# Two more tables and a second chain of scatters for the expert sums of a transformer layer

## The reference, cut to what matters

```python
x = x + layernorm(attention(layernorm(x)))          # 16 query heads, 4 key/value heads, causal
h = layernorm(x).reshape(4096, 256)
topk_w, topk_ids = grouped_topk(h @ gate_w, bias)   # 6 of 64 experts for each token, in 4 of 8 groups
# every expert takes at most 48 tokens (CAP), the earliest ones; the others get nothing from it
buf = zeros((64, 48, 256)).at[expert, slot].set(h[token])
e = silu(einsum('ech,ehf->ecf', buf, w_gate)) * einsum('ech,ehf->ecf', buf, w_up)
out = einsum('ecf,efh->ech', e, w_down)
y = segment_sum(out[expert, slot] * w, token)       # each token adds up what its experts gave it
shared = (silu(h @ ws_gate) * (h @ ws_up)) @ ws_down
x = x + layernorm(y + shared)
```

## Time and profile before

| | |
|---|---|
| median of 3 runs | 2156.44 us |
| the runs | 2150.07, 2156.80, 2156.44 us |
| the profiled execution, its own time | 2158.23 us |
| its span (first to last instruction) | 2156.4 us |
| PE busy | 1927.5 us (89% of the span) |
| DVE, ACT, POOL busy | 1333.7, 1149.5, 1293.5 us |
| attention | 0 to 1861 us |
| `last_quad` | 1861 to 1924 us |
| 32 pairs of experts | 1924 to 2097 us |
| tail | 2097 to 2156 us |

### The profile page before, as it was taken

The page is one execution under the profiler, slowest core; times in us unless marked ns, Lnnn a source line. Parts: engine busy times, 40 slices in busy tenths (PEclk is TensorE's granted clock), DMA queues, the critical chain, the costliest instruction groups (busy, mean ns, idle before and its releaser), DMA issues. The chain is left out here.

```text
span 2156.4 us, 34575 instructions
## 1 busy us (share of the span) xinstructions
PE 1927.5 (89%) x12006; PEld 1631.8 (76%) x12006; DVE 1333.7 (62%) x3172; ACT 1149.5 (53%) x2604; POOL 1293.5 (60%) x1055
## 2 busy tenths in 40 slices
PE   3899999999999999998999999999999999679940
PEld 2788888887788888887888888877888888447730
DVE  1466666666666677676667677766666777642217
ACT  2466665655556565655565655565655555222213
POOL 5666766675657574856585766666666655124533
PEclk9999999999999999999999999999999999885555
DMA  4000000001010100000100100011001000595226
GB/s 168 16 25 21 6 21 6 21 6 46 26 52 1 35 11 21 11 26 30 55 21 6 40 6 25 6 50 35 21 6 40 16 1 11 192 356 170 49 54 210
DMA packets 68587, 103.35 MB, mean 48 GB/s; under 512 B 9350, under 2 KB 49236, under 8 KB 67392
## 3 DMA queue, kind: packets, MB, share of 16 engines
q1 hardware_dynamic: 56816, 84.23, 11.6%
q0 software_dynamic: 7248, 12.72, 2.6%
q10 hardware_dynamic: 4352, 4.20, 0.6%
HBM read 73.47 MB, written 30.04 MB: 48 GB/s over the span
## 5 line engine op out<-in xcount | busy, mean ns | idle before, releaser
L536 PE MATMUL s_ps<-kT,q 128*128 128x512 f32 (+3 forms) x2304 | 596.6, 377 | 11.3 <-ACT probs L900 10.0
L779 DVE TENSOR_TENSOR pT<-t_ps,pT 128x512 fp32r<-128x512 f32 (+3 forms) x768 | 401.5, 550 | 329.8 <-ACT pT L911 328.7
L536 PEld LDWEIGHTS s_ps<-kT,q 128*128 128x128 f32 x2304 | 407.4, 194 | 56.0 <-ACT probs L900 15.7
L561 PE MATMUL av_ps<-pT,v 128*128 128x512 f32 x1728 | 437.1, 399 | 0.0
L1049 POOL TENSOR_TENSOR rope<-raw,sinT 64x512 f32<-64x512 f32 x320 | 411.1, 1285 | 24.6
L766 DVE TENSOR_REDUCE neg_max<-s_ps 128x1 f32<-128x640 f32 (+7 forms) x512 | 383.8, 750 | 65.8 <-PE s_ps L536 59.9
L900 ACT ACTIVATE probs<-s_ps,neg_max 128x640 f32<-128x640 f32 (+7 forms) x512 | 381.6, 745 | 66.5 <-DVE neg_max L766 65.1
L911 ACT ACTIVATE pT<-t_ps 128x512 fp32r<-128x512 f32 (+3 forms) x768 | 348.3, 489 | 127.5 <-PE t_ps L546 122.1
L1046 POOL TENSOR_TENSOR cosed<-raw,cosT 128x512 f32<-128x512 f32 x160 | 206.3, 1290 | 278.4 <-ACT raw L872 270.1
L561 PEld LDWEIGHTS av_ps<-pT,v 128*128 128x128 f32 x1728 | 315.9, 190 | 59.7
L546 PE MATMUL t_ps<-k_ident,probs 128*128 128x128 f32 x2304 | 341.9, 275 | 14.7 <-ACT probs L900 8.2
(11 more groups left out here) (193 smaller groups left out, 1934.6 us busy)
## 6 DMA issues: line engine op xcount, KB each, us to landing
w_early<-in_expert_w SPq DMA_DIRECT2D x5, 2560.0 KB, 29.3
w_staged<-in_wpack SPq DMA_DIRECT2D x47, 256.0 KB, 2.8
w_staged<-in_wpack SPq DMA_DIRECT2D x16, 512.0 KB, 3.6
w_early<-sums SPq DMA_DIRECT2D x16, 512.0 KB, 8.8
e_w_late<-in_expert_w SPq DMA_DIRECT2D x3, 2560.0 KB, 20.3
k_xw<-in_x SPq DMA_DIRECT2D x4, 1024.0 KB, 5.7
k_xb<-in_x SPq DMA_DIRECT2D x4, 1024.0 KB, 5.9
sums<-y POOLq DMA_DIRECT2D x4, 1024.0 KB, 8.7
```

The source lines that it names most:

```text
L536: last = pe.matmul(out, q[:, macro % 2, a, h, int(big)], kT[:, g % 2, s, lo:hi], start=(n == 0), stop=(n == 2))
L561: last = pe.matmul(av_ps[:], v[:, g % 2, a, j], pT[:, s, part_slot(p) + j], start=(j == 0 and n == 0), stop=(j == blocks - 1 and n == 2))
L779: dve.tensor_tensor(lo, t_ps[n % 2][:, 0:count * P].rearrange("p (j n) -> p j n", n=P), hi.bitcast(F32), ALU.subtract).then_inc(t_lo, 1)
```

## The change

- `sums` has four tables. At step `s == 40` of the attention ACT waits for the stores of the zeros and then copies table 1, which is all zeros, to tables 2 and 3 by two DMAs from DRAM to DRAM, 4.24 MB each. SP waits for them at the end of the block.
- Of the first 22 pairs (`TURNS = 11`) the odd ones add to tables 2 and 3, with a semaphore `added[1]` of their own; the even ones and all of the last ten add to tables 0 and 1 (`added[0]`). A scatter waits only for the scatter before it of its own chain. So two scatters can be under way in the first 22 pairs, and one in the last ten. `to_row` takes three instructions for each half instead of one.
- When the eleven odd scatters have landed, SP loads tables 2 and 3 (16 DMAs of 512 KB) while the last ten pairs run, and DVE adds them, one unit in each of its last eight steps (`joined`).
- After the last scatter SP loads tables 0 and 1 as before, 16 DMAs, table 0 now to a part of `w_late` and table 1 to where table 3 lay. POOL adds `m2` (tables 2 and 3) to `m0`; DVE adds `m1` to it, by a linked instruction ahead of the statistics of each unit.
- One semaphore of `w_in` covers two weight loads, so a wait is for 16 experts.

```diff
@@ attention, scalar
+                if s == 40:
+                    act.wait_ge(zeros_out, 16 * (B + 3))
+                    for n in (2, 3):
+                        act.dma_start(sums[n], sums[1]).then_inc(zeros_copied, 16)
...
+TURNS = 11
+
+def in_second(j):
+    return j % 2 == 1 and j < 2 * TURNS
+
+def scattered_earlier(j):
+    return sum(in_second(i) == in_second(j) for i in range(j))
...
@@ last_quad, vector
-            dve.tensor_scalar(index.to_row[0:64], c_ps[1][0:64, 0:EXPERTS // 2], -1.0, FAR, ALU.mult, ALU.add)
-            dve.tensor_scalar(index.to_row[64:128], c_ps[1][64:128, 0:EXPERTS // 2], -1.0, FAR + TABLE, ALU.mult, ALU.add)
+            second, first = slice(1, 2 * TURNS, 2), (slice(0, 2 * TURNS, 2), slice(2 * TURNS, EXPERTS // 2))
+            for i in range(2):
+                half = slice(64 * i, 64 * i + 64)
+                for cols, table in ((second, 2 + i), (first[0], i), (first[1], i)):
+                    dve.tensor_scalar(index.to_row[half, cols], c_ps[1][half, cols], -1.0, FAR + table * TABLE, ALU.mult, ALU.add)
...
@@ experts
-        x1, m0, m1 = (flat[:, i * SIZE:(i + 1) * SIZE].rearrange("p (t n) -> p t n", n=HID) for i in range(3))
+        x1, m2, m3 = (flat[:, i * SIZE:(i + 1) * SIZE].rearrange("p (t n) -> p t n", n=HID) for i in range(3))
+        m0, m1 = w_late[:].rearrange("p e n -> p (e n)")[:, 0:SIZE].rearrange("p (t n) -> p t n", n=HID), m3
+        def landed(j):
+            return added[in_second(j)], 16 * (scattered_earlier(j) + 1)
@@ experts, sync
             sp.wait_ge(y_ready, last_pair(2))
-            sp.wait_ge(added, 16 * PAIRS)
+            sp.wait_ge(added[1], 16 * TURNS)
             for u in range(UNITS):
                 first = u * UNIT * P
+                for dst, table in ((m2, 2 * TABLE), (m3, 3 * TABLE)):
+                    sp.dma_start(unit(dst, u), tiles(sums[table + first:table + first + UNIT * P])).then_inc(loaded[u], 16)
+            sp.wait_ge(y_ready, PAIRS)
+            sp.wait_ge(added[0], 16 * (PAIRS - TURNS))
+            for u in range(UNITS):
+                first = u * UNIT * P
+                sp.wait_ge(joined, u + 1)
                 for dst, table in ((m0, 0), (m1, TABLE)):
                     sp.dma_start(unit(dst, u), tiles(sums[table + first:table + first + UNIT * P])).then_inc(loaded[u], 16)
@@ experts, gpsimd
-                    if j:
-                        pool.wait_ge(added, 16 * j)
+                    if scattered_earlier(j):
+                        pool.wait_ge(added[in_second(j)], 16 * scattered_earlier(j))
...
-                pool.wait_ge(loaded[u], 32)
-                pool.tensor_tensor(unit(m0, u), unit(m0, u), unit(m1, u), ALU.add).then_inc(summed, 1)
+                pool.wait_ge(loaded[u], 64)
+                pool.tensor_tensor(unit(m0, u), unit(m0, u), unit(m2, u), ALU.add).then_inc(summed, 1)
@@ experts, vector
                 if s >= 2:
                     odd(s - 2)
+                u = s - (PAIRS + 2 - UNITS)
+                if u >= 0:
+                    dve.wait_ge(loaded[u], 32)
+                    dve.tensor_tensor(unit(m2, u), unit(m2, u), unit(m3, u), ALU.add).then_inc(joined, 1)
...
             for u in range(UNITS):
                 dve.wait_ge(summed, u + 1)
+                link(dve.tensor_tensor(unit(m0, u), unit(m0, u), unit(m1, u), ALU.add))
@@ experts, vector and scalar, odd(j) and even(j)
-                    wait_ge(added, 16 * (j - Y_RING + 1))
+                    wait_ge(*landed(j - Y_RING))
@@ experts, tensor
-                if (2 * j) % LOADS == 0:
-                    pe.wait_ge(w_in[2 * j // LOADS], 16)
+                if j % LOADS == 0:
+                    pe.wait_ge(w_in[j // LOADS], 32)
@@ build
-    sums = nc.dram_tensor("sums", (2 * TABLE, HID), F32).ap()
+    sums = nc.dram_tensor("sums", (4 * TABLE, HID), F32).ap()
```

More of the change, by code:

```diff
@@ L325, in attention @@
         table_ready, table_read = sem("table_ready"), sem("table_read")
-        zeroed, zeros_out = sem("zeroed"), sem("zeros_out")
+        zeroed, zeros_out, zeros_copied = sem("zeroed"), sem("zeros_out"), sem("zeros_copied")
         kv_in, q_in, o_in = sem("kv_in"), sem("q_in"), sem("o_in")
@@ L453, in _ @@
             sp.wait_ge(weight_out, 32 * (QUADS - 2))
+            sp.wait_ge(zeros_copied, 32)
         @block.tensor
@@ L1255, in _ @@
                 sp.dma_start(w_early[:, n * LOADS:(n + 1) * LOADS],
-                             consts["expert_w"][n * LOADS:(n + 1) * LOADS].rearrange("e p n -> p e n")).then_inc(w_in[n], 16)
+                             consts["expert_w"][n * LOADS:(n + 1) * LOADS].rearrange("e p n -> p e n")).then_inc(w_in[n // 2], 16)
         @block.tensor
@@ L1557, in experts @@
         gu_ready, tanh_done, act_done, h_done = sem("gu_ready"), sem("tanh_done"), sem("act_done"), sem("h_done")
-        y_ready, y_even, y_odd, added = sem("y_ready"), sem("y_even"), sem("y_odd"), sem("added")
+        y_ready, y_even, y_odd = sem("y_ready"), sem("y_even"), sem("y_odd")
+        added, joined = [sem(f"added{n}") for n in range(2)], sem("joined")
         x1_in = sem("x1_in")
@@ L1585, in _ @@
                 at = n * LOADS - EARLY
-                sp.dma_start(w_late[:, at:at + LOADS], consts["expert_w"][n * LOADS:(n + 1) * LOADS].rearrange("e p n -> p e n")).then_inc(w_in[n], 16)
+                sp.dma_start(w_late[:, at:at + LOADS], consts["expert_w"][n * LOADS:(n + 1) * LOADS].rearrange("e p n -> p e n")).then_inc(w_in[n // 2], 16)
             sp.wait_ge(y_ready, last_pair(0))
@@ L1612, in _ @@
                     pool.wait_ge(y_odd, j + 1)
-                    if j:
-                        pool.wait_ge(added, 16 * j)
+                    if scattered_earlier(j):
+                        pool.wait_ge(added[in_second(j)], 16 * scattered_earlier(j))
                     pool.indirect_dma_start(sums, bass.IndirectOffsetOnAxis(to_row[:, j:j + 1], 0), y[:, j % Y_RING], None,
-                                            bounds_check=2 * TABLE - 1, oob_is_err=False, compute_op=ALU.add).then_inc(added, 16)
+                                            bounds_check=4 * TABLE - 1, oob_is_err=False, compute_op=ALU.add).then_inc(added[in_second(j)], 16)
             for u in range(UNITS):
-                pool.wait_ge(loaded[u], 32)
-                pool.tensor_tensor(unit(m0, u), unit(m0, u), unit(m1, u), ALU.add).then_inc(summed, 1)
-            pool.wait_ge(added, 16 * PAIRS)
+                pool.wait_ge(loaded[u], 64)
+                pool.tensor_tensor(unit(m0, u), unit(m0, u), unit(m2, u), ALU.add).then_inc(summed, 1)
+            for n, count in enumerate((PAIRS - TURNS, TURNS)):
+                pool.wait_ge(added[n], 16 * count)
         @block.vector
@@ L1638, in odd @@
                 if j >= Y_RING:
-                    dve.wait_ge(added, 16 * (j - Y_RING + 1))
+                    dve.wait_ge(*landed(j - Y_RING))
                 at = HID + 2 * j + 1
@@ L1695, in even @@
                 if j >= Y_RING:
-                    act.wait_ge(added, 16 * (j - Y_RING + 1))
+                    act.wait_ge(*landed(j - Y_RING))
                 at = HID + 2 * j
@@ L1770, in build @@
         kept = Kept(lambda name, shape, dt=F32: ctx.enter_context(nc.sbuf_tensor("k_" + name, shape, dt)))
-        attention(nc, args, x, wpack, x1_rows, rows, [sums[0:TABLE], sums[TABLE:2 * TABLE]], x2t_rows, kept)
+        attention(nc, args, x, wpack, x1_rows, rows, [sums[n * TABLE:(n + 1) * TABLE] for n in range(4)], x2t_rows, kept)
         index = Index(lambda name, shape, dt=F32: ctx.enter_context(nc.sbuf_tensor("i_" + name, shape, dt)))
         w_early = ctx.enter_context(nc.sbuf_tensor("w_early", [P, EARLY, PACK], F32))
-        w_in = [ctx.enter_context(nc.semaphore(f"w_in{n}")) for n in range(EXPERTS // LOADS)]
+        w_in = [ctx.enter_context(nc.semaphore(f"w_in{n}")) for n in range(EXPERTS // LOADS // 2)]
         last_quad(nc, args, kept, index, rows, x1_rows, x2t_rows, sums[0:TABLE], w_early, w_in)
```

## The result

The changed kernel takes 2160.98 us in the median of 20 runs (2156.18 to 2165.47), the kernel before 2154.91 us in the median of 20 (2150.07 to 2162.50). The ratio is **1.0027, 95% interval 1.0016 to 1.0038**: slower by 0.27%, just inside the 0.3% (the interval reaches beyond it). The span of its profiled execution is 2161.1 us, 4.7 us above that of before.

A forecast was written before the change was run, and what follows sets the result against it. Bound: the scatter-to-scatter chain at about 4.6 us a pair, with PE at 4.18 behind it, and DVE late in the tail. Sum -18.3 + 11.5 + 9.8 + 0.5 + 0.5 = +4.0, 2160.4 us; 8 in 10: 2150 to 2168.

The forecast's parts named there:

- (A): First 22 pairs: with the second chain they run at PE's 4.18 us a pair, scatter 22 starts 18.3 us sooner.
- (B): Last ten pairs: loads of tables 2 and 3 delay scatters by 3.3 us each for 3.5 periods, +11.5 us.
- (D): Last ten pairs: DVE's eight additions find idle time and hardly hold POOL's scatter issues, +0.5 us.
- R1: Rival, last ten pairs: scatters take turns with the loads and lose only 0.94 us each; 2153.3 us, chance 0.24.
- R2: Rival, last ten pairs: loads hold scatters as the `x1` load did, 5.2 us each; 2165.6 us, chance 0.22.
- (C): Tail: DVE's eight further additions of 128x1024, partly hidden in the first four units, cost +9.8 us.
- The walk: Tail, units 0 to 3 stepped through with DVE and POOL holding each other up: unit 3's statistics 3.4 to 5.8 us later.
- (E): Attention step 40: ACT's two issues of the table copies mostly hide in its gaps, +0.5 us.

The follow-up runs named there:

- no_joins: Changed kernel without DVE's eight additions of table 3 beside the last ten pairs, all loads kept: ratio 1.0034 to the kernel before, span 2160.1 us.

## Why the prediction was right

Forecast 2160.4 us against a median of 2156.44, +4.0; measured 2160.98 against 2154.91, +6.1 in the medians, +5.8 by the ratio (+3.4 to +8.2), and +4.7 in the spans. That 2160.4 and 2160.98 lie so close is in part luck: the kernel before came out 1.5 us lower than in its first three runs.

- **(A)**, -18.3: measured 91.94 - 110.22 = -18.3, and 20.4 when undone. PE kept 4.18 us a pair up to pair 26. Scatter 8 was 1.6 us late (1977.45, due at 1942.43 + 33.4 = 1975.9) because of the `x1` load, and the chain had caught up by pair 12, as put.
- **(B)**, +11.5, and **(D)**, +0.5: measured +11.5 for both together, 11.6 when loads and additions are left out, so the sum, +12.0, was right. The split was not. The price of the load per scatter, 3.3 us, was right (3.47, 3.25 and 3.32 us without the longer issues), but three scatters paid it and not three and a half: 10.0 us. The longer issues (2.23, 2.10, 2.64 us) took 2.2 us and not 0.5 (the later landings were 0.6 us shorter together, which makes 11.5): `odd`, from which I argued that they stay at 1.59, has one input in SBUF and wasn't the right likeness for an addition with two. These two errors cancel, as no_joins shows, for a reason that the prediction doesn't have: an issue held up for longer keeps the next scatter out of the load. So the sum for the two is in part luck. The price itself was that of one scatter beside another load, chosen by the size of the pieces, and no run varied that size.
- R1, turns between the queues (landings of 4.7), is refuted by landings and packets, R2 (landings of 9) by the landings.
- **(C)**, +9.8: measured +10.4, and removed it gives back 10.4. From unit 4 on 5.86 - 4.59 = 1.27 a unit, put at 1.3. The walk put the statistics of unit 3 at 3.4 to 5.8 us later in the tail; they came at +36.2 after the last landing instead of +30.8, 5.4 later: POOL got in first at unit 2.
- **(E)**, +0.5: nothing that can be measured (0.9999).
- The remaining 0.9 us of the span's 4.7 is the start: the first scatter at 1942.43 instead of 1941.49, well within what the attention varies.
- The lower end of the range, 2150, takes +8.6 for (C); with (C)'s own lower end of +5.2 the same sum is 2156.4 - 18.3 + 2.5 + 5.2 + 1.0 = 2146.8. The measurement came near neither.

The chances put 0.52 on a change within 0.3%, and that is where the ratio lies, though its interval reaches to 0.38%.

## What to carry to other kernels

A chain of small accumulating DMAs pays for other DMAs by their place: the same 8 MB cost this chain 16.1 us issued just ahead of each scatter, 11.5 all at once, and 2.3 issued right behind each scatter's issue. Where a load was queued first, a scatter paid 3.3 to 3.5 us beside the tables and 5.2 beside `x1`. Before a chain is shortened, look for what its new partner (here PE at 4.18 us against 4.62) leaves to gain, and price the combining of the extra results in the stage that has no slack. Two elementwise streams on DVE and POOL can be interlocked on purpose: with POOL's additions beside DVE instructions that have at most one SBUF input the tail here took 60.4 us instead of 66.5.

## What the runs showed of the hardware that I had not expected

- A scatter of q0 beside a running load of q1 had 8 packets in 3.5 us, in which its data were due from about 2045.5 on, and 172 in the next 1.6, a gather's with them (changed kernel, 2045 to 2048.5 and 2048.5 to 2050.1). The Trainium skill, DMA: Bandwidth & Descriptors, in SWDGE vs HWDGE vs iDMA, says that an engine takes turns between its queues at packet boundaries; for the start of a scatter the trace differs, and the measurement decides. In the second stretch both queues move, which agrees.

```profile
q1 hardware_dynamic: 1213, 1.20, 108.9%
q0 software_dynamic: 8, 0.01, 1.4%
```

```profile
q1 hardware_dynamic: 312, 0.31, 59.8%
q0 software_dynamic: 172, 0.21, 55.3%
```

- A `sem_inc` behind an indirect DMA on POOL let SP start 0.1 to 0.2 us before that DMA's own start; a memset in its place let SP start 1.7 us after it (2054.51, scatter at 2052.78).
- POOL's issue of an indirect DMA that starts while a DVE addition with two SBUF inputs runs takes longer: 2.10 to 2.64 us for the scatters instead of 1.59. An addition that starts 0.26 us or more into the issue holds nothing and isn't held (scatters 26 to 28: issues of 1.55 to 1.57 us, additions of 1.22 and 1.23).
- PE was busy without a gap from 1934 to 2057 us and the granted clock was 0.50, the lower level of 1.2 GHz, throughout (34 us of it in rows 5, and this row of the changed kernel):

```profile
2034.00:2059.00 25.00, 23.62 (x125) 18.30 (x124) 10.74 (x21) 6.32 (x17) 9.02 (x6) 0.50 1.03 324
```
